# Four picked tiles per turn in layer 0 of a graph network instead of five, with the fourth chunk's last tile gathered

## What is computed

```python
h = relu(layernorm(x))
# layer 0, over edge_index = (row, col)
m = concat([h[row], edge_attr_16], axis=1)
m = relu(m @ w1a + b1a) @ w1b + b1b
agg = segment_sum(m, col) / max(segment_sum(1, col), 1)
x = x + (relu(concat([h, agg], axis=1) @ w2a + b2a) @ w2b + b2b)
# layer 1
h = relu(layernorm(x))
x = x + (1 + eps) * h + segment_sum(relu(h[src] + edge_attr_32), dst)
```

## Time and profile before

| | us |
|---|---|
| median of 3 runs | 6166.7 (6165.09 to 6170.27) |
| the profiled execution, its own time | 6167.25 |
| its span, first to last instruction | 6165.2 |
| gathers of layer 0 | 62.93 to 3199.15 |
| gathers of layer 1, first start | 3290.55 |

### The profile page before, as it was taken

How to read it: one execution, slowest core, us unless ns; L and a number is a source line. 1 busy time by engine, 2 the same in 40 slices (tenths; PEclk the granted TensorE clock), 3 DMA queues, 4 the chain that set the end, 5 groups by cost and what they waited for, 6 DMA issues and landing times. The chain is left out here.

```text
span 6165.2 us, 106642 instructions
## 1 busy us (share of the span) xinstructions
PE 5919.7 (96%) x32834; PEld 5085.6 (82%) x32835; DVE 3754.2 (61%) x9052; ACT 4351.2 (71%) x8692; POOL 4544.9 (74%) x4799
## 2 busy tenths in 40 slices
PE   7999999999999999999988999999999999999999
PEld 5887777777777777777777888888888888888888
DVE  6554444444444444444447777777777777777776
ACT  5766666666666666666656777777777777777775
POOL 5777777777777777777755777777777777777776
PEclk9999999999999999999998999999999999999999
DMA  4222222222222222222221222222221222222221
GB/s 116 66 69 65 65 65 67 66 67 65 65 65 68 65 66 65 65 65 68 65 50 45 52 52 51 49 53 53 52 51 48 53 52 52 50 50 52 53 53 41
DMA packets 331462, 367.43 MB, mean 60 GB/s; under 512 B 87161, under 2 KB 256536, under 8 KB 331166
## 3 DMA queue, kind: packets, MB, share of 16 engines
q0 software_dynamic: 152000, 160.05, 13.8%
q1 hardware_dynamic: 46276, 130.67, 6.5%
q10 hardware_dynamic: 133146, 76.25, 4.4%
HBM read 358.17 MB, written 8.46 MB: 59 GB/s over the span
## 5 line engine op out<-in xcount | busy, mean ns | idle before, releaser
L977 PE MATMUL bank<-part_high,owner_hot 125*128 125x448 f32 (+1 forms) x10500 | 4011.6, 382 | 181.3 <-ACT owner_hot L1085 147.9
L977 PE MATMUL bank<-part_low,owner_hot 125*128 125x448 f32 (+1 forms) x10500 | 3897.7, 371 | 0.0
L953 POOL DMA_INDIRECT gathered<-projected_rows,indices x2500 | 2368.5, 947 | 779.2 <-issue 692.6
L953 POOL DMA_INDIRECT gathered<-hidden_rows,indices x2250 | 2151.7, 956 | 693.7 <-issue 576.0
L977 PEld LDWEIGHTS bank<-part_high,owner_hot 125*128 125x128 f32 x10500 | 1980.7, 189 | 414.1 <-ACT owner_hot L1085 162.3
L977 PEld LDWEIGHTS bank<-part_low,owner_hot 125*128 125x128 f32 x10500 | 1979.4, 189 | 197.7 <-issue 0.2
L1080 ACT ACTIVATE owner_hot<-owner_in,minus_piece 125x256 fp32r<-125x256 f32 (+2 forms) x3948 | 1591.6, 484 | 37.9 <-PE bank L977 11.6
L1085 ACT ACTIVATE owner_hot<-owner_hot 125x1792 fp32r<-125x1792 f32 (+1 forms) x750 | 1276.0, 1701 | 23.8
L1218 DVE SCALAR_TENSOR_TENSOR hidden<-window_f,places_now,bank 128x512 f32<-128x512 f32 x1500 | 1101.7, 734 | 121.8 <-PE bank L977 121.4
L1251 DVE TENSOR_TENSOR gathered<-gathered,bank 128x384 f32<-128x384 f32 x625 | 346.0, 554 | 1323.6 <-DMA gathered<-projected_rows,indices 1257.2
L1103 ACT ACTIVATE messages<-bank 128x96 f32<-128x96 f32 x625 | 157.5, 252 | 923.4 <-DVE gathered L1251 917.0
(11 more groups left out here) (125 smaller groups left out, 2478.1 us busy)
## 6 DMA issues: line engine op xcount, KB each, us to landing
owner_in<-owner_rows SPq DMA_DIRECT2D x188, 448.0 KB
edges<-in_edge ACTq DMA_DIRECT2D x124, 400.0 KB
gathered<-projected_rows,indices POOLq DMA_INDIRECT x2500
gathered<-hidden_rows,indices POOLq DMA_INDIRECT x2250, 2.4
hidden<-owner_rows SPq DMA_DIRECT2D x62, 448.0 KB
edges<-in_edge ACTq DMA_DIRECT2D x124, 200.0 KB
projected_rows<-projected SPq DMA_DIRECT2D x25, 168.0 KB
sources<-in_src_cols SPq DMA_DIRECT2D x1, 1562.5 KB, 6.8
```

What stands on the lines that cost most here:

```text
L953: pool.indirect_dma_start(gathered_rows(k, row)[:, t, :], None, table, bass.IndirectOffsetOnAxis(ap=index(k, odd(turn))[:, t:t + 1], axis= ...
L977: last = nc.tensor.matmul(bank[pick_home[home]][:, 0:PITCH * D].rearrange("p (f b) -> p f b", b=PITCH)[:, :, 0:rows.shape[2]], pick_hot(pi ...
```

## The change

Layer 0 picks tile 4 of slots 0, 1, 2 and 4 only. Tile 4 of slot 3 is gathered like its other four. Its 32 rows of `edges` that would hold the picked rows are set to zero once, so that the edge product adds nothing of a node for it, and its five tiles are rectified by one instruction. Batch 1 of the one-hot matrices holds one tile in place of two. Layer 1 keeps its 7 picks.

```diff
-LAYER_PICKS = ((tuple(pick for pick in PICK_TABLE if pick.tile == TILES - 1),) * 2,
-               (PICK_TABLE, PICK_TABLE))
+LAYER_PICKS = ((tuple(pick for pick in PICK_TABLE if pick.tile == TILES - 1 and pick.slot != 3),) * 2,
+               (PICK_TABLE,) * 2)
...
+                    for slot in range(SLOTS):
+                        if all(pick.slot != slot for pick in LAYER_PICKS[0][0]):
+                            for parity in range(2):
+                                nc.vector.memset(edge_t(slot, parity)[PICK_ROW:P, :], 0.0)
...
-                wide_home = [0, 1, 2, 0, 1] * 2
+                wide_home = [0, 1, 2, 0, 1, 2, 0, 1]
...
-                        if n == picks_of(BATCH_SLOTS[BATCH_OF_SLOT[pick.slot]][0], turn)[0]:
+                        if n == min(m for slot in BATCH_SLOTS[BATCH_OF_SLOT[pick.slot]] for m in picks_of(slot, turn)):
...
-                        pe.wait_ge(picks_copied, picks_before(turn) + (picks_of(k, turn)[0] + ROUND + 1))
+                        for n in picks_of(k, turn):
+                            pe.wait_ge(picks_copied, picks_before(turn) + (n + ROUND + 1))
...
-                            nc.scalar.activation(message[k][:, TILES - 1, 0:row],
-                                                 bank[edge_home[k]][:, (TILES - 1) * H1:TILES * H1], ACT.Relu)
+                            if tiles < TILES:
+                                nc.scalar.activation(message[k][:, TILES - 1, 0:row],
+                                                     bank[edge_home[k]][:, (TILES - 1) * H1:TILES * H1], ACT.Relu)
```

## The result

The changed kernel takes 6320.5 us (median of 4 runs, 6319.8 to 6322.5), the kernel before 6166.8 us (4 runs): a ratio of 1.0249, 95% interval 1.0231 to 1.0267. It is slower by 154 us, 2.5%. The profiled execution took 6319.78 us, its span is 6318.0 us.

A forecast was written before the change was run, and what follows sets the result against it. POOL's gather list was taken to bound layer 0, PE as runner-up. 6167.25 + 154.9 (added gather) - 0.6 (smaller ACT batch) = 6321.5 us, forecast 6321 us for the median, 2.5% slower; range 6310 to 6334.

The forecast's parts named there:

- The bound: Layer 0's loop: POOL's gather list, 20 gathers at 1.2488 us making the 24.98 us turn; PE only runner-up.
- The added gather: One more gather per turn in slot 3, paid at the pitch in 124 turns, turn 0 covered: +154.9 us.
- they stay: Start of layer 0: the two other start gaps, 3.58 and 2.69 us, were to remain as they were.
- surplus waits could shift: Start of layer 0: part of the range, up to 6.3 us of surplus waits that could shift.
- The smaller batch on ACT: Halved batch 1 of one-hots: nothing in the loop, but turn 0's 0.94 us gap falls to 0.30: -0.6 us.
- the moved wait: POOL's half-way wait in slot 4, now for slot 4's own pick instead of slot 3's: cost 0.
- The 14 us of room: Time between slot 4's pick half done, near 1509, and POOL's wait in slot 4, at 1523.54.
- The removed pick on PE: PE spared 14 products, 3.02 us, and one transpose, 0.27 us, per turn: worth 0 us.
- Rival B: PE's step 0 is the bound: 3.3 us less per turn, 412 us over 125 turns, 5755 us; chance 2%.
- Rival C: POOL's gap ahead of gathers is elastic: 21 gathers fit the old turn at 1.19 us, 6167 us; chance 2%.
- Rival D: PE's clock falls in new pauses and PE becomes the bound: 1800 us more, 7970 us; chance 2%.
- The rule by occupancy: Layer 0's loop: optimize the highest-occupancy engine first; PE, 80% by weight loads, is above POOL, which gives rival B.

The follow-up runs named there:

- the repeat: The changed kernel run again, unaltered, on chip A: 6319.7 us against 6166.0 us for the kernel before, ratio 1.0250.
- the run that makes PE the bound: Kernel before with the 14 products of slot 3's pick made twice in every turn of layer 0, chip A: 6374.0 us, ratio 1.034.

## Why the prediction was right, point by point

**The bound.** Right. POOL's list bounds layer 0 before and after. With PE's products taken away the time stays (directly on B and C, by the line through 21 and 18 gathers on A); with gathers added or taken away it follows, by 154 us each on chip A.

**The added gather**, 124 x 1.2488 = 154.9 us. Right: the last gather moved by 154.1 us, the kernel by 154. In the long run the distance was 0.3 ns shorter than before, which makes 0.9 us over 2586 gathers. That turn 0's gather is covered was right too: turn 1's first gather still waits 3.43 us for ACT.

**Start of layer 0.** Partly wrong, and small. The gap of 0.94 us did go, as predicted. But "they stay", said of the other two, failed: the changed kernel's gaps are

```profile
94.95 0.94 POOL L957 DMA_INDIRECT gathered<-projected_rows,indices  x1 [3.43 <-ACT messages L1111]
...
102.58 0.94 POOL L957 DMA_INDIRECT gathered<-projected_rows,indices  x1 [2.94 <-ACT messages L1111]
...
117.55 5.94 POOL L957 DMA_INDIRECT gathered<-projected_rows,indices  x1 [0.30 <-issue]
```

Turn 1 begins 1.16 us later than at 93.79. The reason lies ahead of it, in DVE's wait for a DMA of the preparation, here the changed kernel:

```profile
79.81 3.42 DVE L1198 TENSOR_TENSOR destinations<-destinations,hidden 128x3125 f32<-128x3125 int32 x1 [9.23 <-DMA fars<-far_rows]
```

The same instruction starts at 78.48 in the kernel before. The change's two memsets are not the cause: DVE's first instruction on x starts at 4.29 us, against 4.39 before, so its wait for x hid them as predicted. The instruction on the destinations starts at 79.81, 78.91 (the repeat) and 79.03 us (18 gathers) in three executions with the change, at 78.48, 78.26 and 78.12 us in three without it. That is a spread of 1.7 us, which the range had as "surplus waits could shift" and the sum had not; six values do not settle whether the change has a share in it. The books from gather to gather: +1.16 (first), +0.25 (second gap, 2.94 for 2.69), -0.64 (third gap gone), -0.62 (the long gather, 5.94 for 6.56 us), 124 x 1.2488 = +154.9, -0.9 (shorter distance) make 154.1. The four start terms cancel to +0.15, where the sum had -0.6; that they nearly cancel is luck, since only the third was forecast.

**The smaller batch on ACT and the moved wait.** Right: no gap longer than the usual one in mid-layer, only 24 of 2588 gaps that name PE or ACT, all of 0.30 us. The 14 us of room were not touched.

**The removed pick on PE**, 0 us. Right, by both runs that do it alone. The details of what PE would look like were a little off: busy 87% for "at or under 85%"; and the pause after slot 0's scatter is 2.77 us, not 4. The first goes with the clock: the same four picks are busy for 21.1 us of a turn in the kernel with 18 gathers, at a clock of 0.99, and for 22.8 us here, at 0.93. PE's need per turn was read as 24.0 us from its busy share and is 23.6 by the run that makes PE the bound. A likely reason, not tested, is that the tail of a last product ahead of a pause counts as busy, while the next product would otherwise have started in it.

**Rival B (PE is the bound)** had 5755 us and is refuted by the result itself. The removed pick, to which it gave 412 us, was worth none, by the two runs on B and C and by the line on A; the run that does make PE the bound looks different from both kernels. **Rival C (the gap is elastic)** is refuted by the added gather alone and by 18 gathers: the gap stays 0.30 us with PE at 87% as with PE at 94%, and whoever waits. **Rival D (PE's clock falls)**: the clock does fall, once per turn for about 3 us, and the granted mean is 0.93, inside the predicted 0.8 to 1.0. It would need more than 5.5 us of work at the lower level to matter. By PE's need of 23.6 less the pick's 3.3, 20.3 us, the changed kernel has 26.2 - 20.3 = 5.9 us of room.

**The rule by occupancy.** The Trainium skill, "Perfetto Trace Analysis", section "Identifying the Most-Contended Engine", put PE first. The measurement decides against it here: POOL with 76% was the bound, though PE was busy 96% with products and 80% with weight loads. What it overlooks in this kernel is idle time that belongs to each instruction. Counted from start to start, POOL's gathers fill the loop without a rest: 20 x 1.2488 is the turn.

## What to carry to other kernels

Look at the distance between starts, not only at busy time: where an engine's list runs at one constant distance, its gaps are the same whoever is named in them, and its consumer waits, take that engine for the bound whatever its share says, and expect each entry to cost the distance. Before moving work from one engine to another, ask which of the two has gaps that vary; work moved onto the one whose gaps are constant is paid in full, and the relieved engine gives nothing back. To measure how much room the runner-up has, double a known piece of its work until the first engine's gaps grow, as the doubled pick did.

## What the runs showed of the hardware

**Pauses on two chips.** Chips B and C run the same program 1.207 and 1.209 times as long, with layer 0's gathers at a median of 0.944 to 0.947 us. Both layers have pauses of 2 to 3.3 us on POOL after about every tenth gather, mostly ended by "remote", and DVE, ACT and PE have pauses as well. What ends or starts them was not found. A ratio measured there, 1.0234 and 1.0236 for the gather alone, still came out near A's 1.0250.

**A product's clock after a pause.** After 2.77 us without products PE worked about 3 us at a granted clock of 0.50, then at 0.98 again.

**A long gather beside a DVE instruction.** At the start of layer 0 one gather lasts 5.94 us, while DVE works on two arrays of 125 x 4800:

```profile
117.54 5.13 DVE L1208 TENSOR_TENSOR self_part<-self_part,bias_self 125x4800 f32<-125x4800 f32 x1
```

DVE ends at 122.67, the gather at 123.49. In the kernel before the gather stands like this:

```profile
115.53 6.56 POOL L953 DMA_INDIRECT gathered<-projected_rows,indices  x1 [0.30 <-issue]
```

and the DVE instruction like this:

```profile
116.12 5.14 DVE L1202 TENSOR_TENSOR self_part<-self_part,bias_self 125x4800 f32<-125x4800 f32 x1
```

so DVE ends at 121.26 and the gather at 122.09. In both the gather ends 0.8 us after DVE, and so it does in the four other executions on A, by 0.82 or 0.83 us, with gathers of 5.78 to 6.33 us; its length is set by where DVE's instruction falls. In turn 0 a gather beside DVE's 3.42 us over 128 x 3125 shows the same:

```profile
79.32 3.39 POOL L953 DMA_INDIRECT gathered<-projected_rows,indices  x1 [0.30 <-issue]
```

It ends at 82.71, DVE at 81.90. Beside DVE's two reductions of 3.5 us from 62.48 us on, which read one array each, the gathers from 64.35 us on last 0.94 us. The Trainium skill, "SBUF — State Buffer", section "🔬 SBUF: two separate sides", says that DVE and GpSimd share a pair of ports under an exclusive lock, which a DVE instruction with two SBUF inputs takes against a GpSimd operation that reads SBUF, and that the one that comes second waits for the whole instruction of the other. The ends 0.8 us after DVE's agree with it. The gather of the kernel before began 0.59 us ahead of DVE and still waited; either its start in the profile is not when it wants the port, or the order is not settled by who comes first. No run here tells the two apart.
